# The second run of context products is moved from between the projections of K and V to behind V's projection

## The reference, cut to what matters

```
x = x + attn(layernorm(x))            # attn: below
x = x + ffn(layernorm(x))             # silu(x@dq(w1).T) * (x@dq(w2).T), then @dq(w3).T

q, k, v = (h @ w.T + b).reshape(B, S, 32, 32)          # three projections 1024 -> 1024
scores  = einsum('bshd,bstd->bsht', q, k)               # for each token: 32 heads against its own 32 heads
probs   = softmax(scores / sqrt(32))
context = probs @ v                                    # for each token: 32x32 by 32x32
```

## Time and profile before

| | |
|---|---|
| median of three runs | 1895.01 us |
| the profiled execution | 1894.59 us, its span 1892.7 us |
| TensorE, VectorE, ScalarE, GpSimd busy | 97%, 91%, 73%, 66% of the span |
| granted TensorE clock, mean | 0.993 |
| attention stage, steps 0 to 15 | about 66 to 520 us of the span |
| feed-forward stage | from about 520 us to the end |

### The profile page before, as it was taken

How to read it: one execution, slowest core, us unless ns; L and a number is a source line. 1 busy time by engine, 2 the same in 40 slices (tenths; PEclk the granted TensorE clock), 3 DMA queues, 4 the chain that set the end, 5 groups by cost and what they waited for, 6 DMA issues and landing times. The chain is left out here.

```text
span 1892.7 us, 42748 instructions
## 1 busy us (share of the span) xinstructions
PE 1831.2 (97%) x16470; PEld 884.2 (47%) x16470; DVE 1729.0 (91%) x1848; ACT 1378.0 (73%) x1523; POOL 1252.9 (66%) x706
## 2 busy tenths in 40 slices
PE   6899999999989999999999999999999999999998
PEld 6555555555434344444444444444444444444443
DVE  6799999999888999999999999999999999999985
ACT  7233333333359898898998988989989889898881
POOL 0134534534647887977878779778787787787961
PEclk9999999999999999999999999999999999999999
DMA  9346666665587131221122212212211221131115
GB/s 322 123 128 188 169 173 198 170 174 157 133 215 239 41 66 45 45 62 49 44 52 47 56 44 50 61 44 50 61 44 44 50 61 44 44 65 42 39 29 190
DMA packets 252925, 182.76 MB, mean 97 GB/s; under 512 B 177792, under 2 KB 220800, under 8 KB 252800
## 3 DMA queue, kind: packets, MB, share of 16 engines
q1 hardware_dynamic: 221600, 167.28, 31.8%
q10 hardware_dynamic: 31200, 13.64, 3.5%
HBM read 114.29 MB, written 24.12 MB: 73 GB/s over the span
## 5 line engine op out<-in xcount | busy, mean ns | idle before, releaser
L1718 DVE SCALAR_TENSOR_TENSOR bank<-signs,bank 128x1024 f32<-128x1024 int8 (+2 forms) x756 | 919.9, 1217 | 53.2 <-ACT signs L1584 25.8
L1878 PE MATMUL bank<-x2T,w12T 128*128 128x512 f16 x4128 | 896.3, 380 | 8.3 <-DMA x2T<-x_lo_dram 5.9
L1878 PEld LDWEIGHTS bank<-x2T,w12T 128*128 128x128 f16 x4128 | 403.9, 98 | 497.5 <-DMA x2T<-x_lo_dram 6.4
L1584 ACT ACTIVATE signs<-w_first,compare_bias 128x1024 int8<-128x1024 f32 (+1 forms) x588 | 630.6, 1138 | 1.5 <-DVE bank L1718 1.1
L1584 ACT ACTIVATE signs<-w_last,compare_bias 128x1024 int8<-128x1024 f32 (+2 forms) x294 | 314.4, 1119 | 0.8 <-DVE w_first L1718 0.6
L1068 PE MATMUL bank<-wT,xT_hi 128*128 128x512 f16 x768 | 294.8, 384 | 2.4 <-PEq L321 2.4
L1068 PE MATMUL bank<-wT,xT_lo 128*128 128x512 f16 x768 | 294.1, 383 | 2.0 <-issue 2.0
L1906 PE MATMUL bank<-w3T_hi,hT_hi 128*128 128x512 f16 x672 | 255.3, 380 | 7.5 <-DMA w3T_lo<-half 4.7
L1907 PE MATMUL bank<-w3T_lo,hT_hi 128*128 128x512 f16 x672 | 255.4, 380 | 0.0
L1908 PE MATMUL bank<-w3T_hi,hT_lo 128*128 128x512 f16 x672 | 255.4, 380 | 0.0
L1498 POOL TENSOR_TENSOR acc<-acc,hidden 128x512 f32<-128x512 f32 x160 | 201.1, 1274 | 27.5 <-ACT hidden L1625 26.7
(11 more groups left out here) (140 smaller groups left out, 2142.7 us busy)
## 6 DMA issues: line engine op xcount, KB each, us to landing
ff_raw<-in_L_ffn_w SPq DMA_DIRECT2D x63, 512.0 KB, 4.6
w_first<-in_L_ffn_w SPq DMA_DIRECT2D x41, 512.0 KB, 3.8
w_last<-in_L_ffn_w SPq DMA_DIRECT2D x19, 512.0 KB, 4.0
x_nat<-in_L_attn_hidden_states SPq DMA_DIRECT2D x16, 512.0 KB, 5.8
x_res<-in_L_attn_hidden_states SPq DMA_DIRECT2D x16, 512.0 KB, 5.3
x<-x_res SPq DMA_DIRECT2D x16, 512.0 KB, 3.6
acc<-x SPq DMA_DIRECT2D x4, 2048.0 KB, 8.2
out<-acc SPq DMA_DIRECT2D x15, 512.0 KB, 2.6
```

The lines of the kernel that those rows point to most:

```text
L1584: nc.scalar.activation(signs[0:rows, ring(v, k), 0:cols], w_nat(v % SLOTS)[0:rows, 0:cols], ACT.Sign, scale=COMPARE[SUMMED[k]][0], bias=co ...
L1718: V.scalar_tensor_tensor(to, part, HALF_STEP[SUMMED[k]], total, ALU.mult, ALU.add).then_inc(sign_used, 1)
L1878: last = nc.tensor.matmul(dst, w, tokens_of(sb_, x)[:, :, c], start=c == 0 and i == 0, stop=c == C - 1 and i == 2)
```

## The change

The call of `mix_part` for the second half is moved down by one line, from in front of V's projection to behind it.

```diff
                 if project:
                     project_one(n, u, it, 1, with_lo, mix_first if attend else None)
+                    project_one(n, u, it, 2, with_lo, ahead_half if ahead else None)
                     if attend:
                         mix_part(n, HALF, QUAD)
-                    project_one(n, u, it, 2, with_lo, ahead_half if ahead else None)
                 if ahead:
                     next(ahead)
```

## The result

The changed kernel takes 1934.63 us (median of four runs, 1931.89 to 1935.41), the kernel before 1893.61 us (four runs, 1889.67 to 1895.59). The ratio is 1.0217, with a 95% interval of 1.0196 to 1.0237: 2% slower, 41 us. The forecast was 1934 us, and its range holds the result. That says nothing yet of its steps, and one of them turns out to be wrong.

The account below looks back on a forecast made before the run. TensorE and VectorE waiting for each other in a ring with little slack was taken as the bound. 1894.6 + 25 (ring and hiccups) + 14 (clock) = 1934 us; likeliest case 1926 to 1942, eight in ten 1914 to 1953 us.

Parts of the forecast that it names:

- the ring: Attention steps: VectorE's second weighing waits for the moved run, TensorE's next turn for VectorE; 30.65 or 29.6 us a step.
- the two parts of the ring: TensorE from turn to moved run's end, 17.45 us; VectorE from weighing to next turn, 13.15 us behind an even step.
- the joining of the runs: Moved run joins the next run of scores on TensorE: one matmul-size change less, 0.1 us gain per step.
- hiccups: Stops of TensorE's own supply; those in Q and scores hidden by the new gap, 3 us added for context runs.
- slack of 2.6 to 3.6 us: TensorE's standstill ahead of each turn, in place of 0.65 to 0.85 us before the change.
- the forecast's own gaps: 13 new TensorE gaps ahead of the turn; clock falls behind 7, costing turn and K 2.0 us each, 14 us.
- the clock falls in every step: Rival: half clock behind all 13 new gaps, 2.3 us each, 55 us in all, 1950 us; chance 0.23.
- The sum's 22 us for the ring without hiccups: The sum's terms without the clock and the 3 us of hiccups: 1.9, 19.4 and 1.1 us.
- step 2: Its turn comes at 129.6 instead of 127.77, 1.9 us late, after step 1's moved run.
- the twelve turns: Turn of step 2 to turn of step 14: 361.5 against 342.1 us, 19.4 us more, plus 3 us of hiccups.
- step 14: V still held for VectorE's scales; weighing at about 19.9 us behind the turn instead of 18.8, costing 1.1 us.

Follow-up runs that it names:

- e4_apart_fill: e3_apart with the first 12 matmuls of Q's second half run twice in each step, ahead of the turn; 1932.3 us, ratio 1.0201.
- e2_wait_alone: Kernel before, TensorE's order untouched, with one wait added: VectorE's second weighing also waits for V's second half; 1939.33 us, ratio 1.0225.
- e5_join_alone: Kernel before, with both runs of context products joined behind K, ahead of V; 1930.13 us, ratio 1.0188.
- e1_ring_cut: Changed kernel, with VectorE's second weighing and flip_context behind V's second evacuation and norm statistics taken ahead of it; 1927.74 us, ratio 1.0182.
- e3_apart: Changed kernel, with the runs of scores moved between and behind Q's halves so they don't touch the moved run; 1940.72 us, ratio 1.0249.
- e7_apart_late: Changed kernel with e3_apart's order on TensorE and e1_ring_cut's order on VectorE; 1905.28 us, ratio 1.0057.
- e11_spread_late: Changed kernel with each run of 64 products cut into two of 32, eight matmuls apart, and e1_ring_cut's order on VectorE; 1906.66 us, ratio 1.0069.

## Why the prediction was right, and where it was wrong

**Right: VectorE's wait and the ring.** L911 waits for L1124 in 14 steps, 45.3 us; the two parts of the ring, 17.45 and 13.15 us, were measured as 17.46 and 13.13 in step 5. e4_apart_fill shows the turn of the ring whole at 30.70 us, e2_wait_alone that the wait by itself, with TensorE's order of before and with the clock's part, costs 45 us.

**Wrong: the joining of the runs.** The prediction priced it as a gain, one change between small and large matmuls less, 0.1 us a step, and said of hiccups in Q and the scores that the new gap hides them. It had the earlier trace rows before it, with gaps "issue" of up to 1.8 us inside single runs, and took them for accidents of a fixed number: the sum has 3 us for them. They grow with the length of the run. In the twelve steps the gaps "issue" are 8.6 us before, 31.1 us in after (25.4 of them in the scores, in 13 places), 29.8 us in e5_join_alone and 1.4 us with runs of 32. By itself the joining costs 36 us (e5_join_alone) or 34 (e1_ring_cut).

**Wrong by that: where TensorE stands still.** L281 was to wait 2.5 to 4 us in each step from 2 to 14. It waits 4 times, 2.8 us in all, since TensorE has lost its slack of 2.6 to 3.6 us ahead of time, in the scores. The wait forecast is that of e2_wait_alone and e3_apart, 13 and 12 times.

**Wrong by that too: where the clock falls.** It was to fall on turn and K, which the ring can't hide. In after it falls on Q, whose time the ring has to spare until the slack is used up; then TensorE sets the turn, as at 253.58. The turns are not 30.65 and 29.6 us in turn, but from 29.6 to 33.2, 31.1 in the mean. In the twelve turns of after seven gaps have half clock behind them, the number of the forecast, but they are others, in scores and projections, so that the number shows nothing. Where the forecast's own gaps exist, 11 of 13 fall (e2_wait_alone), at 2.1 to 2.4 us each: more than the 7 that it took, and not quite all, as the rival "the clock falls in every step" had it. The sum's 22 us for the ring without hiccups and 11 such gaps would give 45 to 49 us; e2_wait_alone measured 45.

**Why the sum came out.** The two causes are not added, they hide each other: 45 us for the ring alone, 36 for the joining alone, 41 for both. Of the three stretches, step 2 was right (1.8 against 1.9), the twelve turns are 31.0 against 19.4 + 3 + 12 x 14 / 13 = 35.3, step 14 is 3.7 where 1.1 and 14 / 13 were forecast: that taking the run away ahead of V opens the gap of 0.64 us at the first transposition to 2.98, and slows V behind it, was missed. The 1.8 us less ahead of step 1 and the 2.7 us more in the feed-forward stage, in single profiled executions, stay unexplained. The size was right partly by luck: had the two costs, of which it knew one, added up, the time would have been near 1975.

**What the gaps are.** Gaps inside the scores of after, step by step (two more stand in the rows at 211.66 and 242.99, with 83 and 61 matmuls left in the run; the number behind the x is what is left behind the gap):

```profile
274.44 0.59 PE L1110 MATMUL bank<-kT,qT 32*32 32x32 f32 x39 [2.42 <-issue]
...
305.45 0.43 PE L1110 MATMUL bank<-kT,qT 32*32 32x32 f32 x17 [2.17 <-issue]
...
367.38 1.60 PE L1110 MATMUL bank<-kT,qT 32*32 32x32 f32 x101 [3.31 <-issue]
...
398.28 1.29 PE L1110 MATMUL bank<-kT,qT 32*32 32x32 f32 x79 [2.08 <-issue]
...
429.08 0.69 PE L1110 MATMUL bank<-kT,qT 32*32 32x32 f32 x57 [1.94 <-issue]
```

The gap comes 22 matmuls later in every step: 83, 61, 39, 17 left. Then it has left the run behind it, and one that stands 256 instructions earlier comes into the run: 101, 79, 57 left. It hangs on a place in the stream of instructions, then, that is not tied to the work. With their weight loads 22 matmuls are 44 instructions, and a step has 1236 (616 matmuls, 616 weight loads and 4 for semaphores, which the rows leave out), so from a gap to the next one 1280 instructions pass, five times 256. In e5_join_alone the count goes down by 22 a step as well (72, 50, 28, 6), though the gap stands in other work. The Trainium skill (Runtime: NRT & Kernel Launch, section Instruction fetch mechanics) says that instructions are brought in blocks of 16 KiB, which are 256 instructions; five of these are 1280, which fits.

The traces settle it. Counted through TensorE's instructions from the start of the trace, every gap "issue" of over 0.2 us between 85 and 560 us stands at one and the same place of each 256 instructions, behind the 193rd: 10 of 10 in before, 19 of 19 in after, 150 of 150 in all thirteen traces. Gaps that the work of another engine ended stand at any place. The instruction queue's packets (1.64 MB in 100, 16.4 KB each) are the other half: each of the 150 gaps ends 1.2 to 1.7 us after the end of such a packet, and a packet took 0.9 to 2.1 us in after, 1.0 in the median. At the gap of 242.99 the packet runs from 240.64 to 241.71, and TensorE stands still from 240.69 on:

```profile
q8 instruction: 1, 0.02, 13.3%
```

So TensorE waits there for its next block of instructions. By the same section of the Trainium skill crossing into the next block costs little, since it is fetched while the one before is executed. That doesn't hold here, with 31.1 us of gaps in twelve steps: the two joined runs are 512 instructions in 2.5 us, so that a whole block passes in 1.25 us, about the time that one packet takes.

In the earlier trace rows and the five other gaps inside runs of steps 2 to 14 before, 6 to 17 matmuls were left: the place stood near the end of a single run, so that most of a block had passed in it.

**Still open.** What starts a fetch, and how far ahead of its use, the traces don't tell; nor does the length of a gap tell when the clock falls. And neither e7_apart_late nor e11_spread_late came to the time of before: that their last 11 to 12 us are gaps at other places and the price of cuts is read from their waits, not shown by a run.

## What to carry to other kernels

Ahead of moving a run of small matmuls, look at what it will touch, since two runs that come to stand in a row can cost more than the dependence that was looked at; gaps "issue" inside such a run in the trace of before are the warning, and the count left behind the gap tells whether they drift with the instruction stream. Where an engine has to wait, ask what the clock does to the work behind the wait, and which cause will be late first: two losses on one ring hide each other, so that taking away one of them shows little (7 us here), and only each one alone shows its size. A total that agrees is no proof of its terms.

## What the runs showed of the hardware

- A run of 128 products of 32 by 32 in a row (256 matmul rows and as many weight loads, 2.5 us) stopped TensorE for about 2 us in most steps, always at the same place of each 256 instructions of its queue, and each stop ended 1.2 to 1.7 us after a packet of the instruction queue; one of 64 seldom (8.6 us in twelve steps), runs of 32 eight large matmuls apart hardly (1.4 us).
- Behind the gaps ahead of a turn the granted clock was 0.50 in 11 of 13 cases in e2_wait_alone and in 10 of 12 in e3_apart, at 2.1 to 2.4 us each in the former. The length of a gap alone doesn't tell it: behind gaps of 3.77 us (e2_wait_alone, at 161.26) and 1.78 us (after, at 211.66) it stayed at 1.00, behind one of 1.40 us (e4_apart_fill, at 408.06) it fell. Filling such a gap with 2.6 us of useless matmuls in every step made the kernel 8.4 us faster than with the gap.
